# Attention in plain single precision on two 64-row tiles, and half the convolution moved

## The reference

```python
x1 = x + deformable_conv(x_groupnormed)          # 9 taps, bilinear sampling with learned offsets
g  = groupnorm(x1)
# gates and a 4 x 4 matrix per image from the pooled x1: exp, then 20 rounds of
#   M = M / M.sum(-1); M = M / M.sum(-2)         (Sinkhorn; 40 "half-steps")
x2 = x1 + gate * (conv3x3(g) + conv_b) + trace(M) / 4 * g
y  = layernorm(tokens(x2))                       # 256 tokens of 64 channels per image
# causal attention, 8 heads of 64 channels, scale 1/8:
q, k, v = y @ w_qkv ; s = softmax(mask(q @ k.T / 8)) ; t = t + (s @ v) @ w_proj + b_proj
t = t + moe(layernorm(t))       # 8 experts, top 2, GELU
t = t + windowed_attention(layernorm(t))
t = t + moe(layernorm(t))       # 16 experts, top 2, SiLU gate
```

## Time and profile before

| | |
|---|---|
| median of 3 runs | 490.46 us (490.11 to 490.84) |
| the profiled execution | 486.73 us |
| its span, first to last instruction | 484.9 us |
| busy: PE, DVE, ACT, POOL | 434.6, 347.4, 283.1, 175.6 us |
| the chain that ended last, by engine | PE 63%, DVE 16%, ACT 8%, issue 6% |
| granted TensorE clock, mean | 0.982 |

### The profile page before, as it was taken

The page is one execution under the profiler, slowest core; times in us unless marked ns, Lnnn a source line. Parts: engine busy times, 40 slices in busy tenths (PEclk is TensorE's granted clock), DMA queues, the critical chain, the costliest instruction groups (busy, mean ns, idle before and its releaser), DMA issues.

```text
span 484.9 us, 9115 instructions
## 1 busy us (share of the span) xinstructions
PE 434.6 (90%) x2998; PEld 303.3 (63%) x2998; DVE 347.4 (72%) x1090; ACT 283.1 (58%) x676; POOL 175.6 (36%) x305
## 2 busy tenths in 40 slices
PE   2999999999968988979999988999989888998994
PEld 1787777767467887979898944344435444545542
DVE  4178998867777656788978853637666888797862
ACT  3467776732557876758788855765655333343431
POOL 4400001203134563383793342415341454343342
PEclk9998999999989998989999999999999999999998
DMA  7300000000400000012300004212112213041330
GB/s 178 144 2 1 2 0 1 1 2 0 87 3 1 1 2 1 2 39 51 69 20 3 1 3 141 63 39 68 43 38 74 68 45 105 28 122 66 99 102 11
DMA packets 13567, 20.94 MB, mean 43 GB/s; under 512 B 4592, under 2 KB 6384, under 8 KB 13008
## 3 DMA queue, kind: packets, MB, share of 16 engines
q1 hardware_dynamic: 13056, 19.99, 14.4%
q10 hardware_dynamic: 464, 0.37, 0.3%
HBM read 19.62 MB, written 0.72 MB: 42 GB/s over the span
## 4 chain that ended last, share of the span: by engine, by line
PE 63%; DVE 16%; ACT 8%; issue 6%; POOL 4%; DMA 2%; POOLq 0%; DVEq 0%; SPq 0%; ACTq 0%
PE PS L2171 14%; PE PS L1871 7%; PE PS L1909 6%; PE PS L2182 5%; PE PS L2193 5%; PE PS L1930 3%; PE PS L2103 3%; PE PS L2091 2%; PE PS L1829 2%; PE PS L1998 2%; PE PS L2013 2%; PE PS L2047 2%; ACT score_arena L968 2%; DVE QL L1468 2%; DVE score_arena L1577 2%
## 5 line engine op out<-in xcount | busy, mean ns | idle before, releaser
L2171 PE MATMUL PS<-YTs,WH 64*128 64x512 f32 x192 | 77.0, 427 | 1.9 <-ACT VV L1067 1.6
L735 POOL TENSOR_TENSOR pr<-pr 128x512 f32<-128x512 f32 x39 | 50.4, 1291 | 75.9 <-DVE pr L1630 44.7
L2171 PE MATMUL PS<-YX,WH 64*128 64x512 f32 x192 | 77.2, 426 | 0.0
L968 ACT ACTIVATE score_arena<-score_arena,nmx 128x128 f32<-128x128 f32 (+1 forms) x128 | 56.9, 446 | 22.2 <-DVE nmx L1577 21.8
L1067 ACT ACTIVATE VV<-PS 128x512 f32<-128x512 f32 x64 | 35.4, 595 | 41.6 <-PE PS L2171 41.5
L1023 ACT ACTIVATE stage<-PS,wk 128x512 f32<-128x512 f32 x64 | 40.8, 684 | 22.8 <-PE PS L2171 22.7
L1743 DVE TENSOR_TENSOR stage<-VV,PS 128x512 f32<-128x512 f32 x64 | 41.8, 682 | 17.1 <-ACT VV L1067 12.5
L2171 PEld LDWEIGHTS PS<-YTs,WH 64*128 64x128 f32 x192 | 35.3, 184 | 29.6 <-ACT VV L1067 12.6
L908 ACT ACTIVATE st_mem<-PS 128x512 f32<-128x512 f32 x72 | 37.3, 612 | 18.5 <-PE PS L1909 18.5
L2103 PE MATMUL PS<-cst,score_arena 128*128 128x128 f32 x192 | 34.4, 290 | 6.6 <-ACT score_arena L968 6.1
L2091 PE MATMUL PS<-YTs,QH 128*128 128x128 f32 (+1 forms) x128 | 38.9, 328 | 0.0
(11 more groups left out here) (277 smaller groups left out, 1130.1 us busy)
## 6 DMA issues: line engine op xcount, KB each, us to landing
QH<-gate_store SPq DMA_DIRECT2D x96, 128.0 KB, 2.9
stage<-in_wexp SPq DMA_DIRECT2D x6, 512.0 KB, 5.9
wk<-in_w SPq DMA_DIRECT2D x1, 1034.0 KB, 9.8
wa<-in_wat SPq DMA_DIRECT2D x1, 768.0 KB, 8.1
out<-X SPq DMA_DIRECT2D x16, 32.0 KB, 1.9
cst<-in_consts SPq DMA_DIRECT2D x1, 483.0 KB, 6.4
wc<-in_w SPq DMA_DIRECT2D x2, 183.5 KB, 5.8
score_arena<-in_wcv SPq DMA_DIRECT2D x2, 144.0 KB, 6.2
```

Source lines behind the costliest of these rows:

```text
L735: nc.gpsimd.tensor_tensor(acc[:, c % 2], acc[:, c % 2], weighted[:, u % 2], ALU.add).then_inc(acc_added, 1)
L968: ins = nc.scalar.activation(PR[:, s % 3, cols], MS[:, s % 3, cols], ACT.Exp, bias=nmx[:, s % 3, qt:qt + 1], scale=-1.0, accum_out=rsum[:, ...
L2171: ins = mm(PS[:, banks[i], :], w[hs, m, tiles[i] * P:(tiles[i] + 1) * P], ys[i][hs, cs], start=(k == 0), stop=(k == 2))
```

## The change

- Attention works in plain single precision: one set of weights (AV), one q (Q), y stored twice, on rows 0 to 63 and 64 to 127 (YA, of its own). The high and low parts, the second computation of the weights and the remainders on VectorE go. `ln_both` writes both copies of y in one instruction.
- The four score matmuls of two heads are issued together, one head on each half of the rows (`scores(s)` at odd steps for s + 1 and s + 2), into banks 0 and 1; they wait until both banks have been masked. A projection fill covers four heads of q, or both token tiles of v, on the two row halves into banks 6 and 7: three fills an image, each copied by one ScalarE instruction.
- Half 0 of the convolution is done inside the tap loop (`CONV_AT`), into bank 5; half 1 between the first token chunk's steps and in loop steps 0 and 1. Its adds to X1 are done at step 5.
- The second balancing runs wholly in the loop (40 half-steps, reciprocals in steps 1 to 21, the mid one now behind both maskings); its exponential is issued after step 0, its gates on GpSimd at step 0 with the fill `gS` at step 4. `DIAG_AT` is 21, with the trace, residuals, token transposes and layer norm of chunks 2 and 3 two to three steps later than before.
- `gate_wide` gets memory of its own.

```diff
-    return [("q", a, i) for i in range(HPAIRS)] + [("v", a, i) for i in range(PT)]
-
...
-MID_INVERSE, END_INVERSE = [s for s in range(17) if s != 4], [s for s in range(15) if s != 3]
+    return [("q", a, 0), ("q", a, 1), ("v", a, 0)]
+
+
+DIAG_AT, XT_AT, YA_AT = 21, (22, 29), (7, 27, 38)
+DVE_HALVES = 0
+GATES_AT = 4
+POOL_HALVES = tuple(min(40, 2 * s) for s in range(21))
+MID_INVERSE, END_INVERSE = range(2, 22), range(1, 21)
...
-    return {0: (2, 3, 4, 5, 6, 7), 3: (2, 3, 4, 5, 6, 7)}.get(a, (0, 1, 2, 3, 4, 5))
+    return {0: (2, 4, 6), 3: (5, 6, 7)}.get(a, (1, 3, 5))
...
+    if s == GATES_AT:
+        out.append(("gS", 0))
     if s == DIAG_AT:
         out.append(("cB", 0))
-    if s < 2:
-        out.append(("q", 0, 2 + s))
+    if s == 0:
+        out.append(("q", 0, 1))
+    if a + 1 < IMAGES and i in projections_at(a):
+        out.append(projections(a + 1)[projections_at(a).index(i)])
...
-FIRST_PROJECTIONS = [("q", 0, 0), ("q", 0, 1), ("v", 0, 0), ("v", 0, 1)]
+FIRST_PROJECTIONS = [("q", 0, 0), ("v", 0, 0)]
...
-HALVES = (8, 20, 25, 30, 36)
+HALVES = (6, 34, 38)
...
+CONV_AT = (33, 34, 35)
+CONV_SPLIT = (3, 4, 5)
+CONV_STEPS = (6, 8, 9)
...
-        AVH = sb("AVH", 3 * 512, dtype=F32R)
-        AVL = sb("AVL", 3 * 512, dtype=F32R)
-        minus = AVL[:, 0:P]
+        AV = sb("AV", 2 * 512)
...
-        QH = sb("QH", 2, HEADS, S, dtype=F32R)
-        QL = sb("QL", 2, HEADS, S, dtype=F32R)
+        Q = sb("Q", 2, HPAIRS, S)
+        YA = sb("YA", B * S)
+        GW = sb("GW", WIDE * CW)
...
-                    if n == DVE_HALVES:
-                        pool.wait_ge(balanced, 2)
+                    if n == 0:
+                        pool.wait_ge(exp_ready, 2)
...
-            batch_gates(1)
...
+                if s == 0:
+                    batch_gates(1)
...
-            def copy_av(to, ready):
-                nc.scalar.activation(to[:, 0:1024].rearrange("p (a n) -> p a n", a=2), PS[:, 4:6, :], ACT.Copy).then_inc(ready, 1)
-                nc.scalar.activation(to[:, 1024:1536].rearrange("p (a n) -> p a n", a=2), PS[:, 6:8, 0:256], ACT.Copy).then_inc(ready, 1)
-
             act.wait_ge(av_ready, 1)
-            copy_av(AVH, avh_ready)
+            nc.scalar.activation(AV[:].rearrange("p (a n) -> p a n", a=4), PS[:, 1:5, 0:256], ACT.Copy).then_inc(av_copied, 1)
             batch_apply(1)
-            batch_exp(1)
-            act.wait_ge(av_taken, 1)
-            copy_av(AVL, avl_ready)
             nc.scalar.activation(small[:, 40:40 + J], c_("euler"), ACT.Sqrt).then_inc(table_loaded, 1)
             act.wait_ge(lnvar_ready, 1)
             nc.scalar.activation(lnst[:, 1, 0:4], lnst[:, 1, 0:4], ACT.Sqrt).then_inc(ln_sd_ready, 1)
             act.wait_ge(table_loaded, 2)
             nc.scalar.activation(small[:, 44:44 + J], c_("euler"), ACT.Exp).then_inc(table_loaded, 1)
-            batch_bias(1)
...
-                if on_side(name):
-                    act.wait_ge(side_filled, SIDE[name] + 1)
+                act.wait_ge(misc_filled, FILL[name] + 1)
+                if kind == "q":
+                    nc.scalar.activation(Q[:, a % 2, 2 * i:2 * i + 2, :], PS[:, 6:8, 0:S], ACT.Copy).then_inc(misc_free, 1)
                 else:
-                    act.wait_ge(misc_filled, FILL[name] + 1)
-                bank = PS[:, 2 if on_side(name) else 7, :]
...
-                    nc.scalar.activation(VV[:, a % 2, i, :], bank, ACT.Copy).then_inc(side_free if on_side(name) else misc_free, 1)
+                    nc.scalar.activation(VV[:, a % 2], PS[:, 6:8, :], ACT.Copy).then_inc(misc_free, 1)
...
+                    if s == 2:
+                        act.wait_ge(conv_ready, 2)
...
+                    if s == GATES_AT:
+                        batch_bias(1)
...
+                if s == 0:
+                    batch_exp(1)
...
-            half_steps(0, HALVES[2], HALVES[3])
-            copy_square(1)
-            half_steps(0, HALVES[3], HALVES[4])
-            copy_logits(1)
-            half_steps(0, HALVES[4], 2 * SINKHORN)
+            half_steps(0, HALVES[2], 2 * SINKHORN)
...
+            def ln_both(c):
+
+                ts = ln_ready(c)
+                nc.vector.tensor_tensor(Y2[:, ts, 0:2 * C].rearrange("p t (r c) -> p t r c", r=2), Y[:, ts].unsqueeze(2).to_broadcast([P, CHUNK, 2, C]),
+                                        lnst[:, 2, ts].unsqueeze(2).unsqueeze(3).to_broadcast([P, CHUNK, 2, C]), ALU.mult).then_inc(y2_ready, 1)
...
             second_residual(0)
-            half_steps(1, 0, 2)
-            gate_inverse(1)
             take_tokens(0)
             ln_center(0)
             ln_variance(0)
-            ln_out(0, False)
+            copy_square(1)
+            ln_both(0)
             second_residual(1)
-            half_steps(1, 2, 4)
             ln_evac("yA", 0)
-            add_conv(2)
-            add_conv(3)
...
-                                        ALU.subtract).then_inc(side_free if on_side(name) else misc_free, 1)
...
-            for name in FIRST_PROJECTIONS:
-                if name[0] == "q":
-                    query_remainders(name)
-            half_steps(1, 4, DVE_HALVES)
-            take_tokens(1)
...
+                nc.vector.tensor_tensor_reduce(MS[:, s % 3, P:3 * P], PS[:, s % 2, P:3 * P], c_("causal"), -SCALE, 1e30,
+                                               ALU.add, ALU.min, nmx[:, s % 3, 1:2]).then_inc(masked_ready, 1)
                 if s in MID_INVERSE:
                     inverse()
-                nc.vector.tensor_tensor_reduce(MS[:, s % 3, P:3 * P], PS[:, s % 2, P:3 * P], c_("causal"), -SCALE, 1e30,
-                                               ALU.add, ALU.min, nmx[:, s % 3, 1:2]).then_inc(masked_ready, 1)
                 if s >= 1:
                     take_fills(s - 1)
+                if s == 0:
+                    take_tokens(1)
+                    copy_logits(1)
+                if s == 2:
+                    gate_inverse(1)
+                if s == GATES_AT + 1:
+                    add_conv(2)
+                    add_conv(3)
                 if s == DIAG_AT + 1:
                     second_residual(2)
                     second_residual(3)
...
+            def conv(r, lo, hi):
+                pe.wait_ge(g2_ready, 2 * r + 2)
+                if r == 1 and lo == 0:
+                    pe.wait_ge(conv_added, 2)
+                for k in range(lo, hi):
+                    ky, kx = divmod(k, 3)
+                    ins = mm(PS[:, 5, :], w_conv[:, k, :], G2[r][:, :, ky:ky + HH, kx:kx + WW], start=(k == 0), stop=(k == TAPS - 1))
+                if hi == TAPS:
+                    ins.then_inc(conv_ready, 1)
 
...
+                if i in CONV_AT:
+                    if i == CONV_AT[0]:
+                        pe.wait_ge(conv_block_loaded, 32)
+                        pe.wait_ge(x1_tile_ready, 3)
+                    n = CONV_AT.index(i)
+                    conv(0, n * TAPS // len(CONV_AT), (n + 1) * TAPS // len(CONV_AT))
...
+            for part, bank, (stationary, moving) in ((0, 1, ("q", "k")), (1, 3, ("v", "p"))):
                 for g in range(HEADS):
                     odd, hp = divmod(g, HPAIRS)
                     hs = slice(odd * C, (odd + 1) * C)
-                    mm(PS[:, 4 + odd, hp * P:(hp + 1) * P], wa[hs, WAT["q"]][:, hp * P:(hp + 1) * P],
-                       wa[hs, WAT["k"]][:, hp * C:(hp + 1) * C].unsqueeze(1).to_broadcast([C, 2, C]), start=not again or hp == 0, stop=not again)
...
-            conv(0, 0, 4)
+                    ins = mm(PS[:, bank + odd, hp * C:(hp + 1) * C], wa[hs, WAT[stationary]][:, hp * P:(hp + 1) * P],
+                             wa[hs, WAT[moving]][:, hp * C:(hp + 1) * C], start=True, stop=True)
+            ins.then_inc(av_ready, 1)
             pe.wait_ge(x1_tile_ready, J)
             group_means(1)
-            attention_weights(False).then_inc(av_ready, 1)
-            conv(0, 4, 5)
...
-            ins.then_inc(av_taken, 1)
             pe.wait_ge(v3_diag_ready, 1)
             mm(PS[:, 0, 64:66], spread, V3[0:B, 0, BATCHES[0], 0], start=True, stop=True).then_inc(cb_diag_ready, 1)
-            conv(1, 0, 1)
...
             def project(name):
                 kind, a, i = name
-                if not on_side(name):
-                    take(*name)
...
-                ins.then_inc(side_filled if on_side(name) else misc_filled, 1)
+                take(*name)
+                for r in range(2):
+                    rs = slice(r * C, (r + 1) * C)
+                    if kind == "q":
+                        g = 4 * i + 2 * r
+                        ins = mm(PS[:, 6 + r, 0:S], AV[rs, g * C:(g + 2) * C], YA[rs, a * S:(a + 1) * S], start=True, stop=True)
+                    else:
+                        ins = mm(PS[:, 6 + r, :], YA[rs, (2 * a + r) * P:(2 * a + r + 1) * P], AV[rs, 512:1024], start=True, stop=True)
+                ins.then_inc(misc_filled, 1)
...
-            transpose_x(0)
-            conv(1, 1, 6)
...
-
             def scores(s):
```

(39 more changed lines are left out.)

179 lines of the change are left out of this document (55 added, 124 removed).

## The result

The changed kernel takes 503.4 us in the median of four runs (495.5 to 513.3), the kernel before 490.3 beside them. It is slower by 1.3% in its two shorter runs and by 2.7% in the median, where I had said 481.0 and a chance of 0.81 for faster. The spread follows the clock: 495.5 us at a mean granted clock of 0.968, 497.4 at 0.959, 509.4 at 0.929, 513.3 at 0.920. The forecast on that scale was 477.2, so 20.2 us are to be explained.

What follows compares the result with a forecast made beforehand. TensorE bounds the tap loop, dependent work the start, the second balancing early loop steps, a chain over the engines later ones. Gains 8.0 - 4.3 + 5.8 = 9.5 us make 477.2 profiled, 481.0 on the median's scale; range 470 to 489.

Steps and rivals of the forecast that it cites:

- a rival of 0.08: In the loop, TensorE's clock falls in the rests between pairs; 496 us with ten of 31 cold; chance 0.08.
- a cold pair: In the loop, a pair of steps at half clock costs about 1.5 us more; from the seventh the gain is gone.
- Steps 21 to 63: Later loop steps: a chain from one score pair to the next sets 83.3 us instead of 89.1, gain 5.8.
- a q pair: In the loop, two steps with a q projection take 3.98 us, against 2.92 for a plain pair.
- Up to the first score: From the tap loop to the first masking: 9.2 us earlier, 8.0 after 1.2 charged for the clock.
- The half clock: At the first taps and transposes before the loop, TensorE at 1.2 GHz costs 1.2 us, bounds 0 and 2.6.
- The balancing: Steps 0 to 21: 40 half-steps of second balancing at 1.03 us set the pace; 4.3 us are given back.
- Tiles beside each other: Score matmuls of two heads run together on the row halves: 0.64 us a pair, 1.28 one after the other.
- 0.1 for a change of tiling: On TensorE, each change between tilings adds 0.1 us, bounds 0 and 0.28.
- the stage behind the loop: After the loop, the same instructions as before; its length was left unchanged.
- VectorE's relief: Rival: after step 21, VectorE's relief is worth more, 1.76 us a step, balancing excess 1: 470 us; chance 0.17.

Runs made afterwards that it cites:

- e11: Kernel before the change, with constant transposes keeping TensorE busy in the three places where its clock fell: 487.2 us, ratio 0.996.
- e15: Changed kernel with constant transposes holding TensorE's clock, its other work in the change's order: 488.5 us, ratio 0.996 to the kernel before.
- e8: Changed kernel with projections issued ahead of the products with v, and constant transposes where the clock fell: 479.1 us, ratio 0.973 to the kernel before.
- e12: e8 with one 16-column matmul, on 64 or 128 rows, behind the products with v of each odd step: 479.4 us in one run.
- e1: Changed kernel with q and v projections issued ahead of the products with v in odd steps: 486.4 us, ratio 0.989 to the kernel before.
- e6: Changed kernel with four instead of 40 half-steps of second balancing and the constant transposes of e2: 486.7 us, ratio 0.996 to the kernel before.
- e2: Changed kernel with 89 constant transposes where TensorE waited, 40 half-steps kept: 491.6 us, ratio 1.000 to the kernel before.
- e7: Changed kernel with a pair's scores written one tile after the other instead of alternating: 499.3 us (498.1 to 501.1).
- e9: Changed kernel with the copies of the q projections, except the first, on VectorE instead of ScalarE: 505.6 us.

## Why the prediction was wrong, step by step

Start of the wide masking L1554 of steps 0, 21 and 63, and what follows, all from profiled executions; the forecast put on the same scale:

```
                before  e11: before,  forecast  changed  e15: clock  e8: clock
                        clock held                                   and order
first masking    138.6      138.5       130.6    131.8      128.7      128.6
to step 21        47.7       47.3        52.0     56.3       50.2       49.4
to step 63        89.1       87.4        83.3     98.2       95.0       85.3
to the end       209.5      210.8       209.5    209.4      209.7      213.9
span             484.9      484.0       475.4    495.6      483.6      477.2
```

- **The failed step: the clock, left to a rival of 0.08.** I had it fall only after long rests, since it fell after 2.97 us. That misread the kernel before, whose clock fell two more times: at 188, after a rest of 1.80 us, and at 140, after rests of 1.99 and 1.19 (its lines stand below this item). In the changed loop it fell after a rest of 2.14 us (142.95), and held at 0.50 from 146 to 158 with TensorE busy 3.58 to 4.00 of every 4 us; it fell again at 218 to 222, after rests of 0.79, 1.22 and 0.56 us within 8 us. In the old loop it came back within 4 us each time. e15 against the change: 12.0 us of the span, which is more than half of the miss: 3.0 at the start, where 1.2 was charged, 6.1 to step 21, 3.2 behind it. (By the medians it is 14.9 us; the change's two shorter runs lie 7 to 9 above e15's median.) I had weighed a cold pair at 1.5 us and asked for seven of them; I didn't ask whether a cold, slower loop with fewer columns in it might stay cold. The Trainium skill reports a case that spoke against the change, and I didn't weigh it (TensorE: Matmul & The Clock Gate, "A second HAM failure mode: psum-queue depth-cycling"): in a bf16 kernel TensorE rested briefly and often between groups of matmuls, and its clock swung between the two levels. The trace agrees: 0.62 over 139 to 160 and 0.76 over 220 to 240, with no rest over 2.2 us.

```profile
187.59 0.41 PE L1987 MATMUL PS<-cst,X 128*128 128x128 f32 x2 [1.80 <-ACT VV L947]
...
186.00:190.00 4.00, 2.40 (x13) 2.44 (x14) 2.47 (x11) 2.81 (x11) 2.54 (x5) 0.74 0.02 4
138.00:142.00 4.00, 2.64 (x13) 2.44 (x14) 2.57 (x15) 2.36 (x9) 2.23 (x12) 0.76 0.02 6
```

- **Steps 21 to 63: the pair chain, mis-sized.** At full clock it takes 95.0 us where I had 83.3, 11.7 more; this is the second step that failed, and nearly as large. Of a q pair's 4.42 us against 3.98, each of the four intervals up to the copy is 0.10 to 0.12 too short in the forecast: transposes to scores 0.48 (0.37 said), scores to products 0.86 (0.74), products to projection 0.81 (0.71), projection to copy 0.75 (0.63). It isn't the change of tiling (0.11 in e12): the scores alone take 0.73, to a projection in the same tiling (228.90 to 229.63 in e8), where their columns make 0.64; and with one change at 0.11 taken off, transposes and products come to 0.37 and 0.70 (said 0.27 and 0.61). Why a group of matmuls takes 0.1 more than its columns is open. Twenty-one pairs at 0.23 are 4.8, ten or eleven fills at another 0.22 are 2.3. The third part I hadn't priced at all: a fill that follows a projection needs its PSUM bank free, and TensorE stood 4.7 us waiting for ScalarE's copies at its head (the last column below: 2.6, 1.2 and 0.9 us ahead of L1967, L1988 and L1956). By this estimate the three make 11.8, about the 11.7 that are to be explained; no run parts them.

```profile
L1967 PE MATMUL PS<-cst,Y 128*128 128x128 f32 x24 | 4.2, 303 | 2.6 <-ACT Q L934 2.4
L1988 PE MATMUL PS<-sw,YTs 128*128 128x16 f32 x8 | 1.2, 255 | 1.2 <-ACT VV L936 1.2
L1956 PE MATMUL PS<-cst,X 128*128 128x128 f32 x4 | 0.8, 286 | 0.9 <-ACT Q L934 0.8
```

- **What I took as given, and e1 took away**: that the projection stands behind the products with v. I wrote "its copy holds ScalarE and the next exponential queues behind it" and priced it, 1.06 us a q pair, without asking whether it had to. With the projection first 9.7 us go (95.0 to 85.3), and what is left is 2.0 over the forecast.
- **Up to the first score: nearly right.** Taps end at 114.5 (said 113.8), balancing ends at 119.4 (119.3), token copy at 121.7 (121.5). The half clock, charged at 1.2 with bounds 0 and 2.6, took 2.3 of three taps alone (5.09 against 2.84 in e8), and 3.0 of the first masking (e15), over the upper bound. With it held the first masking comes 10.0 us earlier than before, where 9.2 was said for a warm TensorE.
- **The balancing: the round right, its place as the bound wrong, the sum near by luck.** It is 1.03 us a half-step, and at full clock e15 goes from step 0 to 21 in 50.2, 52.0 said. But with four half-steps (e6) the scores of step 20 come 47.1 us after the first, with 40 (e2) 48.0: the pair chain alone makes nearly all of it, at 2.21 a step with a q projection against the balancing's 2.06. In e8, whose q pairs are shorter, the balancing binds: TensorE waits some 0.5 us for the masking at most scores from 153 us on, and the loop's first third is 0.8 us shorter than e15's for all its new order.
- **Tiles beside each other, 0.1 for a change of tiling, the stage behind the loop: right** (e7, e12; 209.4 after the loop as before; 209.4 to 213.9 in the other runs' profiles, by where the clock fell there).
- **VectorE's relief** was real and worth nothing: it waited 14.5 us for scores in steps 21 to 63.

The forecast of 481.0 is near what e8 takes (479.1), by two edits that the change doesn't have, and with errors in the terms that cancel.

What stays open: how the 9.7 us of the new order divide between the earlier copy, the fills that no longer wait (0.5 us left of 4.7) and one change of tiling less on each side (0.2 us a pair); e9 only excludes the copy's engine. And why the clock came back quickly in the old loop and not in the new one isn't shown, only that constant work in the rests holds it.
